# Moving one of two differences of x from VectorE to GpSimd in a residual block of two 3x3 convolutions

## The chip, the core and the metric

One core of a Trainium2 chip runs the whole kernel in one launch. The metric is the device time in microseconds, the median of the runs. Of the engines, TensorE (PE; PEld are its weight loads) multiplies matrices, VectorE (DVE), ScalarE (ACT) and GpSimd (POOL) work element by element, and SyncE (SP) issues most of the transfers. Each engine has an instruction stream of its own; they meet at semaphores only, all of them written by hand in this kernel.

## The reference

The input x is 32 images of 64 channels of 56 x 56 in float32. Both convolutions are 3x3 with padding 1 and 64 channels in and out.

```python
def _bn(x, gamma, beta, mean, var):
    inv = gamma * jax.lax.rsqrt(var + EPS)
    return x * inv[None, :, None, None] + (beta - mean * inv)[None, :, None, None]
identity = x
out = jax.nn.relu(_bn(_conv3x3(x, w1, stride=1), g1, b1, m1, v1))
out = _bn(_conv3x3(out, w2, stride=1), g2, b2, m2, v2)
return jax.nn.relu(out + identity)
```

## The kernel before

**Layout.** The 128 partitions are two row parities times 64 channels: a partition holds 28 row pairs of 56 columns of one channel. x_sb has two buffers (XBUFS), one image each, filled by two transfers (one for each row parity). Each convolution is written in a form that saves products along the columns: the input is turned into four column combinations of half width (28 columns), each is multiplied by its own transformed filter, and the results are combined into even and odd output columns. The four combinations of x are:

- the inner pair, x_inner: even plus odd columns (`sum_x`, L392) and odd minus even columns (`difference_x`, L396);
- the outer pair, x_outer: differences of columns two apart (`outer_x`, L407).

Hidden, the relu of conv1, is turned in the same way into t_inner (`sum_hidden` L440, `difference_hidden` L446) and t_outer (`outer_hidden` L454).

**Precision.** TensorE works on pairs of reduced-precision parts: ScalarE rounds a combination to a high part (`high_x` L547, `high_hidden` L568), VectorE subtracts it for the low part (`split_x` L417, `split_hidden` L462), and three products are summed (hi by w_hi, hi by w_lo, lo by w_hi). Only hidden's difference is multiplied in float32 as it is (t_inner by w_mat, at the matmul line L679). All products go to PSUM by halves of an image; a half has four banks.

**From products to output.** ScalarE copies the bank of the inner difference with the bias into z (`copy_sum`, L577 and L578), VectorE joins it with the other inner bank into the even and odd banks (`join`, L431), TensorE adds the outer products onto them, and ScalarE takes the relu: into hidden for conv1 (`relu_hidden`, L583), into out_sb for conv2 (`relu_out`, L606). The residual is added through x_inner: ScalarE writes half the sum and minus half the difference into the conv2 banks (`residual`, L557) before TensorE adds to them. x_inner has four buffers (TBUFS) for this, x_outer has one.

**Order of the work.** Each engine runs the same numbered steps s. In step s, image s+1 is prepared (sum, difference, outer combination, rounding), conv1 of image s is done, image s-1 goes from hidden to conv2, and image s-2 ends. Inside a step each engine's order is written out by hand, with a semaphore wait ahead of each operation. VectorE's step, cut to its middle:

```python
                if now:
                    join(1, s, 0, (2, s - 2))
                if ahead:
                    sum_x(s + 1, ka)
                if last:
                    split_hidden("t1", s - 1, kl % 2)
                if ahead:
                    difference_x(s + 1, ka)
                if now:
                    join(1, s, 1, (2, s - 2))
                if ahead:
                    outer_x(s + 1, ka)
```

Ahead of these stand the second conv2 join of image s-2 and the three combinations of hidden of image s-1; behind them split_hidden of t_outer, split_x of the inner pair, the first conv2 join of image s-1 and split_x of the outer pair. SP's step loads image s+2 into the buffer that outer_x(s) has read for the last time (it waits for tx_ready["outer"], L317), then stores image s-2. GpSimd works only in the prologue: it clears tiles, scales the filters (`scale_matrix`, L243), builds the inner filters of layer 2 (L214 to L216) and their low part (`low_weights`, L257). ScalarE's `high_x` waits for tx_ready, which `difference_x` increments for the inner pair, and ScalarE's first steps have the high part of layer 2's weights (L250) just ahead of `high_x("inner", 1)`.

Of the kernel before, what the change touches and what calls it, by code (L numbers as in the profile page):

```python
# [1 line left out]

# [5 lines left out]
ALU = mybir.AluOpType  # L45
# [3 lines left out]
XBUFS = 2  # L49
TBUFS = 4  # L50
# [10 lines left out]
def residual_block(nc, x, w1, w2, params, out):  # L61
# [14 lines left out]
    with ExitStack() as ctx:  # L76
# [3 lines left out]
        def sem(name):  # L80
            return ctx.enter_context(nc.semaphore(name))
# [60 lines left out]
            {which: sem(f"{what}_{which}") for which in sets} for what in ("filled", "mat", "whi", "wlo"))  # L142

        tx_ready = {"inner": sem("tx_inner"), "outer": sem("tx_outer")}
        xhi_ready = {"inner": sem("xhi_inner"), "outer": sem("xhi_outer")}
        xlo_ready = {"inner": sem("xlo_inner"), "outer": sem("xlo_outer")}

# [152 lines left out]
        @block.sync  # L300
        def _(sp):
            def store(n, half):
                j0, j1 = HALF2[half]

                wait(sp, out_ready, 2 * n + half + 1)
                for parity in range(2):
                    sp.dma_start(out_rows[n, parity][:, j0:j1, :],
                                 out_sb[parity * C:parity * C + C, half]).then_inc(stored[half], 16)

            sp.dma_start(bn[:], params).then_inc(bn_in, 16)  # L310
            load_parity(sp, 0, 0, 0)
            sp.dma_start(w_raw[2][:], w2).then_inc(w_in[2], 16)

            def step(s, k):
                if not isinstance(s, int) or s + 2 < N:

                    wait(sp, tx_ready["outer"], s + 3 - XBUFS)  # L317
                    for parity in range(2):
                        load_parity(sp, s + 2, k + 2, parity)
                if there_is(s, s - 2):  # L320
                    store(s - 2, 0)
                    store(s - 2, 1)

            run(sp, step)

            for half in range(2):
                sp.wait_ge(stored[half], 32 * N)

        @block.gpsimd
        def _(pool):  # L330


            nc.gpsimd.memset(wmat[1][:], 0.0).then_inc(mat_zeroed, 1)
            nc.gpsimd.memset(x_sb[:, :, :, 0:1], 0.0).then_inc(x_zeroed, 1)
            nc.gpsimd.memset(x_sb[:, :, :, W + 1:W + 2], 0.0).then_inc(x_zeroed, 1)
            for t in (x_hi, x_lo):
                for b in range(2):
                    for row in (0, NQ + 1):
                        nc.gpsimd.memset(t[:, b, :, row, :].bitcast(F32), 0.0).then_inc(zeroed, 1)
            nc.gpsimd.memset(hidden[:], 0.0).then_inc(zeroed, 1)  # L340
            nc.gpsimd.memset(wmat[2][:], 0.0).then_inc(mat_zeroed, 1)


            after, row = chain(pool, bn_step[2]), slice(2 + C, 2 + 2 * C)

            pool.wait_ge(inv_ready, 2)
            newton_step(pool, after, row)
            after(pool.tensor_tensor(inv[:, row], inv[:, row], bn[:, 8 + C:8 + 2 * C], ALU.mult))
            pool.tensor_scalar(inv[:, row], inv[:, row], 0.5, None, ALU.mult).then_inc(scale_ready[2], 1)


            scale_matrix(pool, "inner1")
            scale_matrix(pool, "outer1")


            after = chain(pool, prep[2])

            pool.wait_ge(w_in[2], 16)
            double_inner_filters(pool, 2, after)
            scale_matrix(pool, "all2")  # L360
            low_weights(pool, "all2")

        @block.vector
        def _(dve):
# [22 lines left out]
            def sum_x(n, k):  # L387


                dve.wait_ge(x_in[k % XBUFS], (n - k % XBUFS) * (32 // XBUFS) + 32)  # L390
                wait(dve, res_ready, 2 * (n - TBUFS) + 2)
                nc.vector.tensor_tensor(x_inner[:, k, 0], x_columns(k, 0), x_columns(k, 1), ALU.add)  # L392

            def difference_x(n, k):

                nc.vector.tensor_tensor(x_inner[:, k, 1], x_columns(k, 1), x_columns(k, 0),  # L396
                                        ALU.subtract).then_inc(tx_ready["inner"], 1)

            def outer_x(n, k):

# [63 lines left out]
            def step(s, k):  # L464
                ahead, now, last = there_is(s, s + 1), there_is(s, s), there_is(s, s - 1)
                ka, kl = (k + 1) % 4, (k + 3) % 4
                if is_step(s, N):

                    sum_hidden(N - 1, 0)
                    difference_hidden(N - 1, 0)  # L470
                    outer_hidden(N - 1, 0)
                    sum_hidden(N - 1, 1)
                    join(2, N - 2, 1, before_conv2(N - 2))
                    split_hidden("t1", N - 1, kl % 2, 0)
                    split_hidden("outer", N - 1, kl % 2, 0)
                    outer_hidden(N - 1, 1)
                    difference_hidden(N - 1, 1)
                    split_hidden("t1", N - 1, kl % 2, 1)
                    join(2, N - 1, 0, before_conv2(N - 1))
                    split_hidden("outer", N - 1, kl % 2, 1)  # L480
                    return

                if there_is(s, s - 2):
                    join(2, s - 2, 1, before_conv2(s - 2))
                if last:
                    sum_hidden(s - 1)
                    difference_hidden(s - 1)
                    outer_hidden(s - 1)
# [4 lines that stand above are left out]
                    sum_x(s + 1, ka)  # L493
                if last:
                    split_hidden("t1", s - 1, kl % 2)
                if ahead:
                    difference_x(s + 1, ka)
                if now:
                    join(1, s, 1, (2, s - 2))

# [3 lines that stand above are left out]
                    split_hidden("outer", s - 1, kl % 2)  # L504
                if is_step(s, -1):
                    low_weights(dve, "inner1")
                if ahead:
                    split_x("inner", s + 1, ka)

                if last:  # L510
                    join(2, s - 1, 0, before_conv2(s - 1))
                if is_step(s, -1):
                    low_weights(dve, "outer1")
                if ahead:
                    split_x("outer", s + 1, ka)
# [4 lines left out]
        def _(act):  # L520
# [21 lines left out]
            def high_x(which, n, k):  # L542
                full, places = x_full(which, k)

                act.wait_ge(tx_ready[which], n + 1)
                wait(act, outer[1], 2 * (n - 1))
                nc.scalar.activation(x_part(x_hi, k, places), full, ACT.Copy).then_inc(xhi_ready[which], 1)  # L547

# [240 lines left out]
```

## Time and profile before

| | |
|---|---|
| median of 3 runs | 620.58 us (619.97 to 620.64) |
| span of the profiled execution | 618.4 us |
| granted TensorE clock | 0.99 of full speed over the span |
| TensorE, weight loads | 594.2 us (96%), 540.8 us (87%) |
| VectorE | 585.9 us (95%) |
| ScalarE | 476.4 us (77%) |
| GpSimd | 21.0 us (3%) |
| DMA | 52.26 MB, mean 85 GB/s |

The page gives one profiled execution by its span, from the first to the last instruction on the core; no separate time of that execution is given. The median of the runs stands 2.2 us above that span. A busy share is an average over the whole span. Matmuls overlap in TensorE's pipe, so its share is no measure of how near it is to its peak. In a timeline, the start of an operation and the start of the next one on its engine are nearer together than its duration by some 0.1 us, since the next one's start overlaps the last one's end.

### The profile page before, as it was taken

Reading aid. Unit: us, or ns where it says so; the run is one execution under the profiler, and the core shown is the slowest. Engines: PE = TensorE matmul, PEld = TensorE weight load, DVE = VectorE, ACT = ScalarE, POOL = GpSimd, SP = SyncE. Lnnn points to the kernel's source line nnn. Section 1 sums busy time; section 2 is a strip of 40 time slices with the busy share of each in tenths; the row PEclk is TensorE's granted clock in tenths of the full one; section 3 lists DMA queues with packets and bytes.
Section 4 is the critical chain, followed back from the end, with each engine's and each line's share of the span. In section 5 each row is a group of like instructions: output and inputs, shape, how many; then the busy total and the mean of one; then the engine's idle time right before and its main releaser. Section 6 shows DMA issues by size and latency. Waiting matters only on the chain.

```text
span 618.4 us, 8933 instructions
## 1 busy us (share of the span) xinstructions
PE 594.2 (96%) x2962; PEld 540.8 (87%) x2962; DVE 585.9 (95%) x475; ACT 476.4 (77%) x730; POOL 21.0 (3%) x30
## 2 busy tenths in 40 slices
PE   6779999999999999999999999999999999999996
PEld 2668988999998899898898999889989889899885
DVE  6899999999999999999999999999999999999963
ACT  5677878877787877787887778787778788777874
POOL 7600000000000000000000000000000000000000
PEclk9789999999999999999999999999999999999999
DMA  9445666445656546566645565654655664552125
GB/s 151 52 53 79 89 95 103 83 76 88 94 78 104 93 74 92 78 86 96 104 77 79 86 94 80 104 91 73 93 80 83 99 104 77 79 83 45 29 53 104
DMA packets 232891, 52.26 MB, mean 85 GB/s; under 512 B 232496, under 2 KB 232624, under 8 KB 232880
## 3 DMA queue, kind: packets, MB, share of 16 engines
q1 hardware_dynamic: 230928, 51.42, 54.1%
q10 hardware_dynamic: 1952, 0.70, 0.6%
q8 instruction: 6, 0.10, 0.1%
q14 instruction: 5, 0.04, 0.0%
HBM read 26.42 MB, written 25.69 MB: 84 GB/s over the span
## 4 chain that ended last, share of the span: by engine, by line
PE 52%; DVE 24%; issue 12%; ACT 8%; DVEq 0%; ACTq 0%; POOL 0%
PE psum L679 52%; DVE psum L431 8%; DVE x_lo L417 8%; DVE h_lo L462 6%; ACT out_sb L606 3%; DVE x_outer L407 3%; ACT hidden L583 1%; ACT psum L557 1%; ACT z L577 1%; ACT z L578 1%; ACT x_hi L547 1%; ACT h_hi L568 1%; ACT w_mat L531 0%; POOL g_t L216 0%; DVE x_inner L392 0%
## 5 line engine op out<-in xcount | busy, mean ns | idle before, releaser
L679 PE MATMUL psum<-x_hi,w_hi 128*128 128x420 f32 (+1 forms) x512 | 181.4, 354 | 13.1 <-DVE x_lo L417 8.9
L679 PE MATMUL psum<-x_hi,w_lo 128*128 128x420 f32 (+1 forms) x512 | 179.2, 350 | 0.0
L679 PE MATMUL psum<-x_lo,w_hi 128*128 128x420 f32 (+1 forms) x512 | 178.5, 349 | 0.0
L431 DVE TENSOR_TENSOR psum<-psum,z 128x784 f32<-128x784 f32 (+1 forms) x128 | 127.8, 998 | 16.8 <-ACT out_sb L606 11.8
L679 PEld LDWEIGHTS psum<-x_hi,w_hi 128*128 128x128 f32 x512 | 97.2, 190 | 24.0 <-issue 16.4
L407 DVE TENSOR_TENSOR x_outer<-x_sb 128x1568 f32<-128x1568 f32 x32 | 98.7, 3084 | 0.0
L679 PEld LDWEIGHTS psum<-x_hi,w_lo 128*128 128x128 f32 x512 | 97.4, 190 | 0.9
L679 PEld LDWEIGHTS psum<-x_lo,w_hi 128*128 128x128 f32 x512 | 97.2, 190 | 0.9
L679 PE MATMUL psum<-t_inner,w_mat 128*128 128x392 f32 x256 | 94.7, 492 | 1.1 <-ACT psum L557 1.1
L606 ACT ACTIVATE out_sb<-psum 128x784 f32<-128x784 f32 x64 | 57.2, 894 | 48.6 <-PE psum L679 48.5
L577 ACT ACTIVATE z<-psum,bias 128x392 f32<-128x392 f32 (+1 forms) x128 | 75.6, 590 | 23.8 <-PE psum L679 21.2
L679 PE MATMUL psum<-h_lo,w_hi 128*128 128x392 f32 x256 | 87.3, 341 | 0.0
L679 PE MATMUL psum<-h_hi,w_hi 128*128 128x392 f32 x256 | 87.2, 341 | 0.0
L679 PE MATMUL psum<-h_hi,w_lo 128*128 128x392 f32 x256 | 87.0, 340 | 0.0
L583 ACT ACTIVATE hidden<-psum 64x56 f32<-64x56 f32 (+2 forms) x128 | 61.1, 504 | 18.7 <-PE psum L679 18.3
L578 ACT ACTIVATE z<-psum,bias 128x392 f32<-128x392 f32 (+1 forms) x128 | 75.5, 590 | 0.0
L679 PEld LDWEIGHTS psum<-t_inner,w_mat 128*128 128x128 f32 x256 | 47.9, 188 | 19.4 <-issue 1.4
L557 ACT ACTIVATE psum<-x_inner 128x392 f32<-128x392 f32 x128 | 59.3, 503 | 5.0 <-DVE psum L431 3.7
L679 PE MATMUL psum<-t_hi,w_hi 128*128 128x392 f32 x128 | 62.8, 491 | 0.0
L454 DVE TENSOR_TENSOR t_outer<-hidden 128x1624 f32<-128x1624 f32 (+2 forms) x33 | 59.5, 1803 | 0.0
L462 DVE TENSOR_TENSOR h_lo<-t_outer,h_hi 128x1624 fp32r<-128x1624 f32 (+2 forms) x33 | 59.0, 1787 | 0.3 <-ACT h_hi L568 0.3
L417 DVE TENSOR_TENSOR x_lo<-x_outer,x_hi 128x1568 fp32r<-128x1568 f32 x32 | 57.5, 1798 | 0.0
(69 smaller groups left out, 751.0 us busy)
## 6 DMA issues: line engine op xcount, KB each, us to landing
out_dram<-out_sb SPq DMA_DIRECT2D x128, 196.0 KB, 3.3
x_sb<-x_dram SPq DMA_DIRECT2D x63, 392.0 KB, 6.6
x_sb<-x_dram ACTq DMA_DIRECT2D x1, 392.0 KB, 7.2
w_raw<-w_dram ACTq DMA_DIRECT2D x1, 288.0 KB, 4.1
w_raw<-w_dram SPq DMA_DIRECT2D x1, 288.0 KB, 8.4
bn<-params_dram SPq DMA_DIRECT2D x1, 132.0 KB, 3.6
```

The source lines that it names most:

```text
L407: nc.vector.tensor_tensor(x_outer[:].rearrange("p s j q -> p j q s"), rows[:, :, 0:W].rearrange("p j (q s) -> p j q s", s=2), rows[:, :, 2 ...
L417: nc.vector.tensor_tensor(x_part(x_lo, k, places), full, x_part(x_hi, k, places).bitcast(F32), ALU.subtract).then_inc(xlo_ready[which], 1)
L431: nc.vector.tensor_tensor(psum[:, half, EVEN:ODD + 1, 0:width], t1, z[:, half, :, 0:width], ALU.add).then_inc(joined[conv], 1)
L454: nc.vector.tensor_tensor(t_outer[:, :, rows], hid_cols[:, :, rows, 0:WQ], hid_cols[:, :, rows, 1:WQ + 1], ALU.subtract).then_inc(th_ready ...
L462: nc.vector.tensor_tensor(lo, full, hi.bitcast(F32), ALU.subtract).then_inc(hlo_ready[which], 1)
L547: nc.scalar.activation(x_part(x_hi, k, places), full, ACT.Copy).then_inc(xhi_ready[which], 1)
L557: ins = nc.scalar.activation(psum[:, half, bank, 0:width], x_inner[:, k, i, j0:j1, :].rearrange("p j q -> p (j q)"), ACT.Copy, scale=share)
L577: nc.scalar.activation(z[:, half, 0, 0:width], t2, ACT.Identity, bias=bias[:, conv - 1:conv])
L578: nc.scalar.activation(z[:, half, 1, 0:width], t2, ACT.Identity, bias=bias[:, conv - 1:conv], scale=-1.0).then_inc(z_ready[conv], 1)
L583: return nc.scalar.activation(hid_data[rows, :, pairs, 0:WQ], sums[rows], ACT.Relu)
L606: nc.scalar.activation(out_sb[:, half].rearrange("p j (q s) -> p s j q", s=2), psum[:, half, EVEN:ODD + 1, 0:(j1 - j0) * WQ].rearrange("p ...
L679: ins = nc.tensor.matmul(psum[:, half, bank, 0:width], w[:, i, far, :], moving, start=not onto and at == 0, stop=at == len(todo) - 1, skip ...
```

## The change

GpSimd computes the difference of the inner pair of x for every image, VectorE only the sum. GpSimd's difference waits for the image's load and for the residual of the image four back, and increments a new semaphore, difference_ready. VectorE's sum now increments tx_ready["inner"]. ScalarE's rounding of the inner pair waits for both, and so does SP's load into the x buffer (there, for the outer combination and for the difference). On GpSimd the difference of image 0 stands between the scalings of the inner and of the outer filters of layer 1, and the others follow behind all of its prologue.

```diff
@@ -142,6 +105,7 @@
             {which: sem(f"{what}_{which}") for which in sets} for what in ("filled", "mat", "whi", "wlo"))
 
         tx_ready = {"inner": sem("tx_inner"), "outer": sem("tx_outer")}
+        difference_ready = sem("difference_ready")
         xhi_ready = {"inner": sem("xhi_inner"), "outer": sem("xhi_outer")}
         xlo_ready = {"inner": sem("xlo_inner"), "outer": sem("xlo_outer")}
 
@@ -315,6 +279,7 @@
                 if not isinstance(s, int) or s + 2 < N:
 
                     wait(sp, tx_ready["outer"], s + 3 - XBUFS)
+                    wait(sp, difference_ready, s + 3 - XBUFS)
                     for parity in range(2):
                         load_parity(sp, s + 2, k + 2, parity)
                 if there_is(s, s - 2):
@@ -349,9 +314,16 @@
             pool.tensor_scalar(inv[:, row], inv[:, row], 0.5, None, ALU.mult).then_inc(scale_ready[2], 1)
 
 
+            def difference_x(n, k):
+
+                pool.wait_ge(x_in[k % XBUFS], (n - k % XBUFS) * (32 // XBUFS) + 32)
+                wait(pool, res_ready, 2 * (n - TBUFS) + 2)
+                pool.tensor_tensor(x_inner[:, k, 1], x_columns(k, 1), x_columns(k, 0),
+                                   ALU.subtract).then_inc(difference_ready, 1)
+
             scale_matrix(pool, "inner1")
+            difference_x(0, 0)
             scale_matrix(pool, "outer1")
-
 
             after = chain(pool, prep[2])
 
@@ -359,6 +331,12 @@
             double_inner_filters(pool, 2, after)
             scale_matrix(pool, "all2")
             low_weights(pool, "all2")
+
+            def step(s, k):
+                if there_is(s, s + 1) and not is_step(s, -1):
+                    difference_x(s + 1, (k + 1) % 4)
+
+            run(pool, step)
 
         @block.vector
         def _(dve):
@@ -389,12 +367,8 @@
 
                 dve.wait_ge(x_in[k % XBUFS], (n - k % XBUFS) * (32 // XBUFS) + 32)
                 wait(dve, res_ready, 2 * (n - TBUFS) + 2)
-                nc.vector.tensor_tensor(x_inner[:, k, 0], x_columns(k, 0), x_columns(k, 1), ALU.add)
-
-            def difference_x(n, k):
-
-                nc.vector.tensor_tensor(x_inner[:, k, 1], x_columns(k, 1), x_columns(k, 0),
-                                        ALU.subtract).then_inc(tx_ready["inner"], 1)
+                nc.vector.tensor_tensor(x_inner[:, k, 0], x_columns(k, 0), x_columns(k, 1),
+                                        ALU.add).then_inc(tx_ready["inner"], 1)
 
             def outer_x(n, k):
 
@@ -493,8 +467,6 @@
                     sum_x(s + 1, ka)
                 if last:
                     split_hidden("t1", s - 1, kl % 2)
-                if ahead:
-                    difference_x(s + 1, ka)
                 if now:
                     join(1, s, 1, (2, s - 2))
 
@@ -543,6 +515,8 @@
                 full, places = x_full(which, k)
 
                 act.wait_ge(tx_ready[which], n + 1)
+                if which == "inner":
+                    act.wait_ge(difference_ready, n + 1)
                 wait(act, outer[1], 2 * (n - 1))
                 nc.scalar.activation(x_part(x_hi, k, places), full, ACT.Copy).then_inc(xhi_ready[which], 1)
```

**VectorE, the middle of step 2** (the first in the loop). x_inner<-x_sb are the sum (L392) and the difference (L396), psum<-psum,z the joins of conv1, t_lo the low part of hidden's sum. Before:

```order
L431 TENSOR_TENSOR psum<-psum,z 128x2x420 [waits out_ready,inner1]
L390 ISA
L173 ISA [waits x_in1]
L392 TENSOR_TENSOR x_inner<-x_sb 128x784 [waits res_ready]
L462 TENSOR_TENSOR t_lo<-t_inner,t_hi 128x812 [waits hhi_t1]
L396 TENSOR_TENSOR x_inner<-x_sb 128x784
L426 REGISTER_ALU
L427 ISA [waits z1_ready]
L431 TENSOR_TENSOR psum<-psum,z 128x2x392 [waits out_ready,inner1]
L173 REGISTER_ALU
L407 TENSOR_TENSOR x_outer<-x_sb 128x784x2 [waits xlo_outer]
```

With the change (line numbers of the new file, where the sum is L370, the join L405, the outer combination L381):

```order
L405 TENSOR_TENSOR psum<-psum,z 128x2x420 [waits out_ready,inner1]
L368 ISA
L137 ISA [waits x_in1]
L370 TENSOR_TENSOR x_inner<-x_sb 128x784 [waits res_ready]
L436 TENSOR_TENSOR t_lo<-t_inner,t_hi 128x812 [waits hhi_t1]
L400 REGISTER_ALU
L401 ISA [waits z1_ready]
L405 TENSOR_TENSOR psum<-psum,z 128x2x392 [waits out_ready,inner1]
L137 REGISTER_ALU
L381 TENSOR_TENSOR x_outer<-x_sb 128x784x2 [waits xlo_outer]
```

The second x_inner<-x_sb is gone between t_lo and the second join; all else keeps its order, and no wait of VectorE is new.

**GpSimd, from its first weight scaling on.** w_mat<-w_mat,inv is scale_matrix, g_sum and g_t are layer 2's inner filters, w_lo is low_weights. Before:

```order
L243 TENSOR_TENSOR w_mat<-w_mat,inv 128x512 [waits scale1_ready,filled_inner1]
L243 TENSOR_TENSOR w_mat<-w_mat,inv 128x2x256 [waits scale1_ready,filled_outer1]
L214 TENSOR_TENSOR g_sum<-w_raw 128x192 [waits w2_in]
L215 TENSOR_TENSOR g_t<-g_sum,w_raw 128x192 [waits prep2]
L216 TENSOR_TENSOR g_t<-g_sum,w_raw 128x192
L243 TENSOR_TENSOR w_mat<-w_mat,inv 128x1024 [waits scale2_ready,filled_all2,prep2]
L257 TENSOR_TENSOR w_lo<-w_mat,w_hi 128x1024 [waits whi_all2]
```

With the change (x_inner<-x_sb, L321 of the new file, is the difference):

```order
L207 TENSOR_TENSOR w_mat<-w_mat,inv 128x512 [waits scale1_ready,filled_inner1]
L321 TENSOR_TENSOR x_inner<-x_sb 128x784 [waits x_in0]
L207 TENSOR_TENSOR w_mat<-w_mat,inv 128x2x256 [waits scale1_ready,filled_outer1]
L178 TENSOR_TENSOR g_sum<-w_raw 128x192 [waits w2_in]
L179 TENSOR_TENSOR g_t<-g_sum,w_raw 128x192 [waits prep2]
L180 TENSOR_TENSOR g_t<-g_sum,w_raw 128x192
L207 TENSOR_TENSOR w_mat<-w_mat,inv 128x1024 [waits scale2_ready,filled_all2,prep2]
L221 TENSOR_TENSOR w_lo<-w_mat,w_hi 128x1024 [waits whi_all2]
L321 TENSOR_TENSOR x_inner<-x_sb 128x784 [waits x_in1]
L321 TENSOR_TENSOR x_inner<-x_sb 128x784 [waits x_in0]
```

The difference of image 0 stands behind the first scaling, those of images 1 and 2 behind w_lo, and 29 more follow, one for each later image; each waits for its image's x_in, and from image 4 on for res_ready too.

## Rows read from the trace of the kernel before

**Rows 1.** the page, busy time, share and instructions of each engine

```profile
PE 594.2 (96%) x2962; PEld 540.8 (87%) x2962; DVE 585.9 (95%) x475; ACT 476.4 (77%) x730; POOL 21.0 (3%) x30
```

**Rows 2.** waits of VectorE, 100 to 560 us: us in total, times, longest

```profile
DVE psum L431 <- ACT out_sb L606: 8.3, 25, 0.4
```

**Rows 3.** groups of VectorE, 45 to 540 us: busy, mean ns, idle before

```profile
L417 DVE TENSOR_TENSOR x_lo<-x_inner,x_hi 128x1568 fp32r<-128x1568 f32 x27 | 48.0, 1778 | 0.0
...
L396 DVE TENSOR_TENSOR x_inner<-x_sb 128x784 f32<-128x784 f32 x27 | 26.4, 979 | 0.0
```

**Rows 4.** timeline of VectorE, one image: start us, us, what, idle before

```profile
298.61 0.98 DVE L431 TENSOR_TENSOR psum<-psum,z 128x784 f32<-128x784 f32 x1 [0.34 <-ACT out_sb L606]
299.50 3.02 DVE L407 TENSOR_TENSOR x_outer<-x_sb 128x1568 f32<-128x1568 f32 x1
...
309.26 1.01 DVE L440 TENSOR_TENSOR t_inner<-hidden 128x812 f32<-128x812 f32 x1
310.17 1.02 DVE L446 TENSOR_TENSOR t_inner<-hidden 128x812 f32<-128x812 f32 x1
311.09 1.87 DVE L454 TENSOR_TENSOR t_outer<-hidden 128x1624 f32<-128x1624 f32 x1
312.85 1.06 DVE L431 TENSOR_TENSOR psum<-psum,z 128x840 f32<-128x840 f32 x1
...
315.58 1.00 DVE L396 TENSOR_TENSOR x_inner<-x_sb 128x784 f32<-128x784 f32 x1
316.94 0.98 DVE L431 TENSOR_TENSOR psum<-psum,z 128x784 f32<-128x784 f32 x1 [0.35 <-ACT out_sb L606]
```

**Rows 5.** timeline of ScalarE in the same image

```profile
313.94 0.92 ACT L557 ACTIVATE psum<-x_inner 128x392 f32<-128x392 f32 x2
315.93 0.90 ACT L606 ACTIVATE out_sb<-psum 128x784 f32<-128x784 f32 x1 [1.07 <-PE psum L679]
```

**Rows 6.** timeline of TensorE's weight loads in the same image

```profile
306.91 0.19 PEld L679 LDWEIGHTS psum<-x_hi,w_hi 128*128 128x128 f32 x1 [0.48 <-issue]
...
315.56 0.19 PEld L679 LDWEIGHTS psum<-t_inner,w_mat 128*128 128x128 f32 x1
```

**Rows 7.** x_sb on SP, 303.3 to 304.5 us: load of the second half, its landing

```profile
L295 SPq DMA_DIRECT2D x_sb<-x_dram x1: 809/809/809, 303.5 to 303.5; - x1
...
DMA to landing us min/median/max: 6.6/6.6/6.6
```

**Rows 8.** timeline of GpSimd, the prologue

```profile
11.15 5.26 POOL L243 TENSOR_TENSOR w_mat<-w_mat,inv 128x512 f32<-128x512 f32 x2
...
19.48 1.04 POOL L216 TENSOR_TENSOR g_t<-g_sum,w_raw 128x192 f32<-128x192 f32 x1
...
27.00 2.41 POOL L257 TENSOR_TENSOR w_lo<-w_mat,w_hi 128x1024 fp32r<-128x1024 f32 x1 [2.01 <-ACT w_hi L250]
```

**Rows 9.** timeline of VectorE, the prologue and first steps

```profile
10.88 1.00 DVE L396 TENSOR_TENSOR x_inner<-x_sb 128x784 f32<-128x784 f32 x1
11.80 3.78 DVE L407 TENSOR_TENSOR x_outer<-x_sb 128x1568 f32<-128x1568 f32 x1
...
19.98 2.18 DVE L417 TENSOR_TENSOR x_lo<-x_outer,x_hi 128x1568 fp32r<-128x1568 f32 x1
...
26.75 0.98 DVE L431 TENSOR_TENSOR psum<-psum,z 128x784 f32<-128x784 f32 x1
27.63 4.54 DVE L407 TENSOR_TENSOR x_outer<-x_sb 128x1568 f32<-128x1568 f32 x1
...
35.45 1.00 DVE L440 TENSOR_TENSOR t_inner<-hidden 128x812 f32<-128x812 f32 x1
```

**Rows 10.** timeline of ScalarE, the first steps

```profile
26.87 1.52 ACT L547 ACTIVATE x_hi<-x_inner 128x1568 fp32r<-128x1568 f32 x1
28.29 0.93 ACT L583 ACTIVATE hidden<-psum 64x56 f32<-64x56 f32 x2
...
33.74 1.01 ACT L583 ACTIVATE hidden<-psum 64x56 f32<-64x56 f32 x2
```


## The prediction

> **What bounds the kernel now.** I read the busy shares first [rows 1]: TensorE 594.2 us and VectorE 585.9 us of a 618.4 us span, so either could be the bound. The waits of VectorE from 100 to 560 us [rows 2] decide more: in each of 25 images its psum join waited for ScalarE's out_sb, 8.3 us in all. An engine that waits in every image is not what sets the time alone. Then I followed one image. It takes 18.33 us (join at 298.61, the same join at 316.94) [rows 4]. The idle time of VectorE, 0.35 us, stands just before that join (conv1, second half), and the difference to be taken away, 1.00 us at 315.58, stands just ahead of the idle time. The join waits for relu_out, which ran 315.93 to 316.83 on ScalarE [rows 5], and relu_out waited for TensorE. After the join VectorE runs x_outer, h_lo, x_lo and the conv2 join without a pause; TensorE waits for that join, with a gap of 0.48 us at 306.91 [rows 6]. So the loop is TensorE, relu_out, join, x_outer and what follows, TensorE. The difference isn't in it.
>
> **What is removed.** One VectorE operation per image, 0.98 us [rows 3], 0.9 us from its start to the next one. Its cover is the wait for relu_out: with it gone, VectorE could start the join at 315.58 and would wait for 316.94 all the same. Value: zero. What VectorE gets is room, 1.36 us between 315.58 and 316.94. The semaphore of the inner pair moves onto the sum, still on VectorE, at no cost.
>
> **What is added: a reader beside VectorE.** The new operation waits for x_in of its own image and for res_ready of an image four back. Nothing else holds it, so GpSimd runs a whole step ahead of VectorE: at the moment a load lands. The load goes out when x_outer is through; its second half was issued at 303.5 and landed 6.6 us later, at 310.1 [rows 7]. That is 0.05 us before VectorE's difference of hidden at 310.17, while the sum of 309.26 still runs [rows 4]. A little earlier or later makes no matter: each of sum, difference and outer_hidden (309.26 to 312.96) reads two SBUF tiles.
>
> Do the two engines get in each other's way? The prologue shows it [rows 8, 9]. While GpSimd had its two scalings of 512 columns in hand (5.26 us together), x_outer took 3.78 us instead of 3.02. While it had w_lo (27.00, 2.41 us), x_outer took 4.54. While it had 192-column operations, x_lo took 2.18 us instead of 1.78 [rows 3]. And GpSimd waits in its turn: a tiny operation of 192 columns is 1.04 us long at 19.48. So they take turns, an operation at a time, and VectorE loses the whole reading time of each GpSimd operation that gets in between.
>
> How long is that for 784 columns? Three rows:
> - 192 columns: 2.18 - 1.78 = 0.40 us, 2.1 ns a column; for 784, 1.63 us.
> - 1024 columns: reading began by 27.00 and x_outer (start 27.63) lost 1.52, so it ended near 29.15: 2.15 us, 2.1 ns a column; for 784, 1.65 us. By the whole recorded 2.41 us it would be 1.85.
> - 512 columns, one operand a repeated row of 64: 3.78 - 3.02 = 0.76 us; for 784, 1.16 us.
>
> The new operation has two full operands, as the first two have: I take **1.65 us**, with 1.16 and 1.85 as ends. The Trainium skill (GPSIMD Engine Reference, 3.1 Elementwise) gives 4497 ns for a two-operand add of 2048 columns; as an estimate that is 1.72 us here, and with it the sum below would be 2 us more. The trace's 2.1 ns a column agrees within 5%.
>
> **What 1.65 us does to a step.** It falls ahead of outer_hidden, thus ahead of the first conv1 join (312.85) [rows 4]. Three roads lead on from there:
> - VectorE itself, to the second conv1 join: 1.36 us of room (above).
> - ScalarE: residual waits for the first conv1 join (ended 313.91, residual 313.94 to 314.86), and relu_out stands behind it. It could have started at 314.79, operations on ScalarE overlapping by some 0.07 us, and started at 315.93 [rows 5]: room 1.14.
> - TensorE: its fp32 products wait for residual. They began at 315.56 [rows 6], 0.64 us after they could (314.86 and 0.06 for the semaphore). Behind them TensorE has the gap of 0.48 us. Room 0.64 + 0.48 = 1.12.
>
> The shortest room counts: 1.65 - 1.12 = 0.53 us a step. Images 4 to 31 are loaded in steady steps, 28 of them: 28 x 0.53 = **14.8 us**.
>
> **The start.** In the prologue GpSimd has a queue of its own, and the change puts image 0's difference between two weight scalings and image 1's behind all its weight work.
> - With no difference at 10.88, x_outer(0) starts there, holds the reading to 13.8, and the first scaling, which got in at 11.8, is 2.0 us late. The difference of image 0 adds 1.65. VectorE is idle for some of it, and the work of 192 columns (its last at 19.48) ends about 1.1 us late [rows 8, 9].
> - So w_lo asks at 28.1 instead of 27.00, just after x_outer(1) has begun (27.9); x_outer holds to 30.8, w_lo runs to about 33.1, the difference of image 1 to 34.9.
> - x_hi inner on ScalarE, at 26.87 before, waits for that to 34.9 and holds up all behind it: relu_hidden at 28.29, x_hi outer, the second relu_hidden (33.74 before; 34.9 + 1.4 + 0.9 + 1.4 = 38.7 now) [rows 10]. VectorE's first sum of hidden, 35.45 before [rows 9], follows x_lo of the outer pair (38.7 to 40.5): 5.0 us late. The removed difference (-0.9) and image 3's (which meets the unhindered join and then the sum of x, +0.8) nearly cancel.
>
> I take **4.9 us**. Lower end: if w_lo still ran at 27.00 to 29.4, difference 1 would end at 31.2 and the second relu_hidden start at 35.0, 1.3 us late. SP's new wait costs nothing beyond this: from image 2 on GpSimd is done a whole step before x_outer, which SP waits for anyway. The end of the kernel has no x work: zero.
>
> **Sum.** 14.8 + 4.9 = 19.7 us on the profiled span of 618.4, that is 638.1; the median of 620.58 lies 2.2 us above that span, so **640.3 us**. Ends: 1.16 us lies on the room of 1.12, so 28 x 0.04 = 1 and 1.3 make 623; 1.85 gives 28 x 0.73 = 20.4, and with 6 us at the start 647.
>
> **The rivals.**
> 1. *Faster: VectorE is the bound.* For it: 95% busy, and TensorE's gap stands where it waits for a VectorE join. If the 0.89 us came through in every image, it could give at most TensorE's gap, 29 x 0.48 = 13.9 us: 620.6 - 13.9 = 606.7. It needs the GpSimd reads to cost nothing and relu_out to come earlier. Against it: the join waited for out_sb in all 25 images looked at, behind the place of the removal. It decides from a reading time under 0.3 us, and the rows say 0.76 or more. 4%.
> 2. *The reading is covered.* If the landing fell 2 us later, GpSimd would get in behind outer_hidden, beside the conv1 join, which reads one tile in SBUF and one in PSUM. w_lo at 27.00 began during such a join (26.75), which wasn't lengthened. VectorE would lose 1.65 - 0.94 = 0.71, less than the room, and so too with a reading time near 1.16: only the start remains, 620.6 + 1.3 to 4.9 = 622 to 626. The Trainium skill (SBUF — State Buffer, Who interferes with whom) says that an instruction of VectorE with at most one SBUF input doesn't contend with GpSimd; the trace agrees, 0.98 us for the join. Against it: the landings sit at 10.6 us behind x_outer's start, and outer_hidden's end 13.4 behind it. 14%.
> 3. *GpSimd is slower than its dense rows.* x is read in steps of two elements, which no row shows on GpSimd. At 2.2 us reading, 28 x 1.08 = 30 and 6 for the start: 657. 12%.
> 4. *GpSimd never gets between back-to-back VectorE operations* and only starts in VectorE's gaps or joins. It has a whole step in hand, so this is rival 2's time, 622 to 626. Against it: operations of 192 columns did get in between x_lo and w_lo. 5%.
>
> **The numbers.** The forecast, 630 to 648, has 65%; 3 and what lies above, 12%; 2 and 4, 19%; 1, 4%. The likeliest is 640.3. The range of 8 in 10 takes in most of the covered cases and not much of rival 3: 624 to 649. Over 0.2% (1.2 us, about what a measurement of this kernel can tell from no change) slower: 92%; within it: 4%, the low end of the covered cases; faster: 4%.
>
> **What the profile would show.** Right: GpSimd's operations some 10.7 us behind each start of x_outer, each next to a VectorE operation of 2.5 to 3.5 us where it was 1.0 or 1.87; an image of about 18.85 us; waits of TensorE for residual (psum by ScalarE) where there was hardly one; the first sum of hidden near 40 us. Wrong: images of 18.3 us with unstretched operations (rivals 2, 4), or under 18.3 (rival 1); a stretch over 2 us (rival 3).

## Result and profile after

The changed kernel takes 629.44 us (median of 4 runs, 629.09 to 629.80) against 620.50 for the kernel before (4 runs). The ratio is 1.0147, 95% interval 1.0133 to 1.0162: slower by 8.9 us, where 19.7 was forecast. The span of the profiled execution went from 618.4 to 627.0 us, 8.6 more.

The page of the changed kernel, and the waits of all engines from 100 to 560 us:

```profile
PE 592.7 (95%) x2962; PEld 540.5 (86%) x2962; DVE 587.6 (94%) x443; ACT 474.8 (76%) x730; POOL 99.3 (16%) x62
```

```profile
POOL x_inner L321 <- DMA x_sb<-x_dram: 400.4, 25, 17.5
ACT psum L531 <- DVE psum L405: 28.4, 21, 1.5
...
PE psum L653 <- ACT psum L531: 7.3, 20, 0.4
DVE psum L405 <- ACT out_sb L580: 4.5, 5, 0.9
```

VectorE's busy time has not fallen [rows 1]: it has 32 operations fewer, and 587.6 us against 585.9. The wait for out_sb, 25 times in rows 2, comes 5 times. TensorE waits for ScalarE's psum (the residual) 20 times; before, it never did in this stretch.

One image on VectorE, and GpSimd beside it:

```profile
305.73 3.02 DVE L381 TENSOR_TENSOR x_outer<-x_sb 128x1568 f32<-128x1568 f32 x1
...
316.47 1.00 DVE L420 TENSOR_TENSOR t_inner<-hidden 128x812 f32<-128x812 f32 x1
317.39 3.14 DVE L428 TENSOR_TENSOR t_outer<-hidden 128x1624 f32<-128x1624 f32 x1
320.45 1.03 DVE L405 TENSOR_TENSOR psum<-psum,z 128x840 f32<-128x840 f32 x1
...
324.25 3.04 DVE L381 TENSOR_TENSOR x_outer<-x_sb 128x1568 f32<-128x1568 f32 x1
```

```profile
316.47 2.35 POOL L321 TENSOR_TENSOR x_inner<-x_sb 128x784 f32<-128x784 f32 x1 [16.17 <-DMA x_sb<-x_dram]
```

The x_outer of 305.73 is followed by the next at 324.25, 18.52 us on. GpSimd's operation starts 10.74 us after x_outer did, as its load lands, in the same instant as VectorE's difference of hidden. It waits for that one's end, and t_outer, the next on VectorE, takes 3.14 us instead of 1.87 [rows 4]: 1.3 us longer, the reading of 784 columns. Of the 29 images loaded in steps, 20 stretch t_outer so, 2 the difference of hidden (2.3 us instead of 1.0). In the other 7 GpSimd waits for the end of t_outer, reads beside the conv1 join, which keeps its length, and only 0.4 us is left for the sum of x (1.33 to 1.38 instead of 0.96). One of these:

```profile
279.59 1.02 DVE L420 TENSOR_TENSOR t_inner<-hidden 128x812 f32<-128x812 f32 x1
280.50 1.87 DVE L428 TENSOR_TENSOR t_outer<-hidden 128x1624 f32<-128x1624 f32 x1
282.26 1.06 DVE L405 TENSOR_TENSOR psum<-psum,z 128x840 f32<-128x840 f32 x1
283.20 1.36 DVE L370 TENSOR_TENSOR x_inner<-x_sb 128x784 f32<-128x784 f32 x1
```

```profile
279.87 3.86 POOL L321 TENSOR_TENSOR x_inner<-x_sb 128x784 f32<-128x784 f32 x1 [16.38 <-DMA x_sb<-x_dram]
```

The moment of the landing doesn't tell the two kinds apart. By the profile GpSimd's operation began 0.41 to 0.92 us ahead of t_outer in the 20 images that stretch it, and 0.63 to 0.93 us ahead of it in 6 of the 7 others (in the seventh, image 3 at the start, t_outer already ran). So GpSimd, though it asked in time, was sometimes passed over at t_outer's start; what decides it is open.

Where the 8.6 us came in is read from x_outer, 32 times in each kernel (its line's first and last start; the third start from the timeline):

```profile
L381 DVE TENSOR_TENSOR x_outer<-x_sb x32: 2907/3021/3060, 10.8 to 582.6; 128x1568 f32<-128x1568 f32 x32
```

```profile
47.28 3.02 DVE L381 TENSOR_TENSOR x_outer<-x_sb 128x1568 f32<-128x1568 f32 x1
```

The third x_outer starts at 47.28, before at 43.55: **3.7 us at the start**. The last starts at 582.6, before at 573.9: 29 images took 535.3 us instead of 530.3, 18.46 each instead of 18.29: **5.0 us in the steady steps**. The 22 images with a stretched operation carry nearly all of it: they take 18.50 us in the mean, 0.21 more each, 4.6 us in all.

The start itself:

```profile
11.07 3.47 POOL L207 TENSOR_TENSOR w_mat<-w_mat,inv 128x512 f32<-128x512 f32 x1
...
27.66 5.03 POOL L221 TENSOR_TENSOR w_lo<-w_mat,w_hi 128x1024 fp32r<-128x1024 f32 x1 [2.04 <-ACT w_hi L214]
32.65 2.94 POOL L321 TENSOR_TENSOR x_inner<-x_sb 128x784 f32<-128x784 f32 x2
```

```profile
34.23 1.51 ACT L521 ACTIVATE x_hi<-x_inner 128x1568 fp32r<-128x1568 f32 x1 [6.65 <-POOL x_inner L321]
```

The first scaling (L207) waited for x_outer(0), 11.07 to 14.54. w_lo (L221) waited for x_outer(1), 5.03 us long instead of 2.41 [rows 8]. The two differences behind it are through at 34.1 and 35.6, and ScalarE's x_hi, at 26.87 before [rows 10], started at 34.23, with 6.65 us idle ahead of it.

### The profile page after: what moved, and what is told of

It is laid out like the page before. It is cut to its first block, busy times and chain, and to the rows that moved or that the text cites. A ratio compares the mean times of both kernels' runs of the same rounds, so it can differ in the third digit from the quotient of the medians.

```text
span 627.0 us, 9030 instructions
## 1 busy us (share of the span) xinstructions
PE 592.7 (95%) x2962; PEld 540.5 (86%) x2962; DVE 587.6 (94%) x443; ACT 474.8 (76%) x730; POOL 99.3 (16%) x62
## 4 chain that ended last, share of the span: by engine, by line
PE 76%; ACT 7%; DVE 7%; issue 5%; POOL 1%; DVEq 0%; ACTq 0%; POOLq 0%
PE psum L653 76%; DVE psum L405 4%; ACT z L551 2%; ACT psum L531 2%; ACT z L552 2%; DVE x_lo L391 1%; DVE x_outer L381 1%; DVE h_lo L436 1%; ACT x_hi L521 0%; ACT out_sb L580 0%; POOL w_mat L207 0%; POOL x_inner L321 0%; POOL g_t L180 0%; DVEq L401 0%; DVE t_inner L414 0%
## 5 line engine op out<-in xcount | busy, mean ns | idle before, releaser
L653 PE MATMUL psum<-x_hi,w_hi 128*128 128x420 f32 (+1 forms) x512 | 179.6, 351 | 14.8 <-DVE x_lo L391 13.9
L321 POOL TENSOR_TENSOR x_inner<-x_sb 128x784 f32<-128x784 f32 x32 | 76.4, 2390 | 451.1 <-DMA x_sb<-x_dram 451.1
L405 DVE TENSOR_TENSOR psum<-psum,z 128x784 f32<-128x784 f32 (+1 forms) x128 | 127.5, 996 | 15.6 <-ACT out_sb L580 8.6
L653 PE MATMUL psum<-t_inner,w_mat 128*128 128x392 f32 x256 | 96.4, 499 | 9.4 <-ACT psum L531 9.4
L381 DVE TENSOR_TENSOR x_outer<-x_sb 128x1568 f32<-128x1568 f32 x32 | 96.6, 3019 | 0.0
L428 DVE TENSOR_TENSOR t_outer<-hidden 128x1624 f32<-128x1624 f32 (+2 forms) x33 | 85.4, 2587 | 0.0
L653 PEld LDWEIGHTS psum<-t_inner,w_mat 128*128 128x128 f32 x256 | 46.4, 188 | 34.3 <-issue 14.5
L391 DVE TENSOR_TENSOR x_lo<-x_inner,x_hi 128x1568 fp32r<-128x1568 f32 x32 | 57.3, 1791 | 6.3 <-ACT x_hi L521 6.3
```

The source lines that it names most:

```text
L321: pool.tensor_tensor(x_inner[:, k, 1], x_columns(k, 1), x_columns(k, 0), ALU.subtract).then_inc(difference_ready, 1)
L381: nc.vector.tensor_tensor(x_outer[:].rearrange("p s j q -> p j q s"), rows[:, :, 0:W].rearrange("p j (q s) -> p j q s", s=2), rows[:, :, 2 ...
L391: nc.vector.tensor_tensor(x_part(x_lo, k, places), full, x_part(x_hi, k, places).bitcast(F32), ALU.subtract).then_inc(xlo_ready[which], 1)
L405: nc.vector.tensor_tensor(psum[:, half, EVEN:ODD + 1, 0:width], t1, z[:, half, :, 0:width], ALU.add).then_inc(joined[conv], 1)
L428: nc.vector.tensor_tensor(t_outer[:, :, rows], hid_cols[:, :, rows, 0:WQ], hid_cols[:, :, rows, 1:WQ + 1], ALU.subtract).then_inc(th_ready ...
L653: ins = nc.tensor.matmul(psum[:, half, bank, 0:width], w[:, i, far, :], moving, start=not onto and at == 0, stop=at == len(todo) - 1, skip ...
```

## Experiments

Each is compared with the kernel before, run on the same chip. Edits are shown by their main lines, against the changed kernel unless said otherwise. "Mean image" is the mean distance from the third x_outer to the last.

### The removal alone

```diff
 (against the kernel before; images 0 to 2 only)
-                if ahead:
+                if is_step(s, -1) or is_step(s, 0) or is_step(s, 1):
                     difference_x(s + 1, ka)
```

From image 3 on the sum increments the semaphore of the inner pair in the difference's place.

> The kernel before, with VectorE's difference of x computed for images 0 to 2 only; buffer 3 of x_inner's difference is cleared once, and every later image uses what stands in its buffer (output wrong by that, matrix work the same). GpSimd does nothing new. This is the removal alone. Theory (the difference stands in the wait for relu_out, so the removal is worth nothing): as before, within 0.2% (619.5 to 621.5), an image 18.3 us, VectorE idle about 1.2 us ahead of the second conv1 join. Rival (VectorE is the bound and 0.9 us an image comes back): 607 to 612.

Measured: 619.69 us against 620.25, ratio 0.9991 (0.9982 to 1.0000). Its waits of VectorE, 100 to 560 us, and the join on its timeline:

```profile
DVE psum L434 <- ACT out_sb L609: 30.0, 25, 1.2
```

```profile
316.66 0.98 DVE L434 TENSOR_TENSOR psum<-psum,z 128x784 f32<-128x784 f32 x1 [1.21 <-ACT out_sb L609]
```

The wait for out_sb has grown from 0.35 to 1.21 us [rows 4], and the image is 18.3 us as before. The 0.9 us went into that wait. Taking the difference off VectorE is worth 0.6 us here, and the interval reaches from nothing to 1.1 us.

### Where the two costs are

Images 0 and 1 back on VectorE, GpSimd from image 2 on:

```diff
-            difference_x(0, 0)
 ...
-                if there_is(s, s + 1) and not is_step(s, -1):
+                if is_step(s, 1):
+                    pool.wait_ge(difference_ready, 2)
+                if there_is(s, s + 1) and not (is_step(s, -1) or is_step(s, 0)):
 ...
+                if is_step(s, -1) or is_step(s, 0):
+                    difference_first(s + 1, ka)
                 if now:
                     join(1, s, 1, (2, s - 2))
```

> The changed kernel, with the differences of images 0 and 1 back on VectorE in their old place; GpSimd does images 2 to 31. Theory (two costs: 3.7 us at the start from the place in GpSimd's queue, 5.0 us from the reading in steady steps): 629.4 - 3.7 = 625.7, x_outer of image 2 near 43.5 us again, steady images still 18.46 us. Rival (the start is hidden later, all comes from the steady steps): 629.

Measured: 626.24 us, ratio 1.0098 (1.0083 to 1.0114). The third x_outer started at 43.95, the mean image was 18.47 us. The start's cost is gone, the steady one has stayed.

GpSimd's reading moved to where VectorE waits:

```diff
                 wait(pool, res_ready, 2 * (n - TBUFS) + 2)
+                wait(pool, hlo_ready["t1"], n - 1)
```

> The changed kernel, with one more wait on GpSimd: the difference of image n starts only when VectorE is done with t_lo (low part of hidden's sum) of image n-2, so that it reads while VectorE waits for relu_out, 1.36 us of room for a reading of 1.30. Theory (only the place of the reading costs): steady images back to 18.28 us, the start's 3.7 us stay, 624.3. Rival (a GpSimd operation beside VectorE costs wherever it is): 629 or more.

Measured: 624.49 us, ratio 1.0069 (1.0055 to 1.0082); third x_outer at 46.92, mean image 18.32 us. One operation beside the other, VectorE and GpSimd:

```profile
300.53 1.02 DVE L437 TENSOR_TENSOR t_lo<-t_inner,t_hi 128x812 fp32r<-128x812 f32 x1
302.80 0.98 DVE L406 TENSOR_TENSOR psum<-psum,z 128x784 f32<-128x784 f32 x1 [1.25 <-ACT out_sb L581]
303.69 3.01 DVE L382 TENSOR_TENSOR x_outer<-x_sb 128x1568 f32<-128x1568 f32 x1
```

```profile
301.63 1.49 POOL L322 TENSOR_TENSOR x_inner<-x_sb 128x784 f32<-128x784 f32 x1 [16.68 <-DVE t_lo L437]
```

GpSimd reads from 301.63 to about 302.9, in VectorE's pause and the first 0.1 us of the join, and nothing on VectorE is stretched. The same work on the same engines costs nothing there; the images from the fifth x_outer on take 18.29 us, as before the change.

Both edits:

> Both edits: images 0 and 1 on VectorE, and GpSimd's later ones behind t_lo. Theory: both costs gone, 620.5 within 1.2, nothing gained by the change even then. Rival (VectorE as the bound): under 616. Rival (a third cost): 623 or more.

Measured: 620.23 us against 620.25, ratio 1.0002 (0.9993 to 1.0011). The two costs account for the whole change, and with both gone nothing has been gained.

### The room

Half of the rows for GpSimd, the other half on VectorE in the old place:

```diff
-                pool.tensor_tensor(x_inner[:, k, 1], x_columns(k, 1), x_columns(k, 0),
+                pool.tensor_tensor(x_inner[:, k, 1, 0:NQ // 2], x_columns(k, 1)[:, 0:NQ // 2], x_columns(k, 0)[:, 0:NQ // 2],
```

> The changed kernel, with GpSimd taking 14 of the 28 row pairs of each difference and VectorE the other 14 in the old place. Theory (a reading costs only beyond 1.12 us of room): the reading is some 0.7 us, steady images 18.28 to 18.30 us, and of the start's 3.7 us some 2.5 to 3.2 are left: 623 to 624. Rival (the cost follows the work of GpSimd): half of 8.9 us, 625; rival (whatever VectorE loses is lost): above 626.

Measured: 623.18 us, ratio 1.0047 (1.0031 to 1.0064), mean image 18.29 us. VectorE's timeline has t_outer stretched to 2.49 us:

```profile
314.40 2.49 DVE L431 TENSOR_TENSOR t_outer<-hidden 128x1624 f32<-128x1624 f32 x1
```

This is so in 13 of the 27 images between the 4th and the 31st x_outer; in the others GpSimd read beside the join. The 13 take 18.30 us, the others 18.27, the kernel before 18.29: a loss of 0.65 us ahead of the first conv1 join costs no time. The remaining 3.3 us are the start (third x_outer at 46.83).

Each difference twice:

```diff
+                wait(pool, difference_ready, n)
+                pool.tensor_tensor(spare[:], x_columns(k, 1), x_columns(k, 0), ALU.subtract)
                 pool.tensor_tensor(x_inner[:, k, 1], x_columns(k, 1), x_columns(k, 0),
```

> The changed kernel, with each difference computed twice by GpSimd, first into a spare tile (with a wait for its own operation before), then into its place. Theory (turns by whole operations; one with a PSUM operand doesn't take part): the first reading stretches hidden's difference or t_outer by 1.30, the second waits for the end of t_outer and reads beside the first conv1 join, so that only 0.4 of it falls on the sum of x; loss 1.3 + 0.4 = 1.7 an image, 0.6 beyond the room, 17 us, and about 6 at the start: 642 to 645. Rival (the join takes part too, or both readings count): 2.6 - 1.12 = 1.5 an image, 660 to 670.

Measured: 639.69 us, ratio 1.0320 (1.0302 to 1.0337), 2 to 5 us under the forecast of my theory and far from the rival's. VectorE in one image:

```profile
324.81 1.85 DVE L431 TENSOR_TENSOR t_outer<-hidden 128x1624 f32<-128x1624 f32 x1
...
327.51 1.34 DVE L373 TENSOR_TENSOR x_inner<-x_sb 128x784 f32<-128x784 f32 x1
328.78 2.29 DVE L439 TENSOR_TENSOR t_lo<-t_inner,t_hi 128x812 fp32r<-128x812 f32 x1
```

In 25 of 28 images the first reading ran beside the conv1 join and took 0.36 from the sum of x, the second took 1.30 from t_lo: 1.66 us an image, as expected, in other places than expected. The mean image was 18.65 us, 0.37 over the one before where I had counted 0.6. That fits a loss behind the first conv1 join, which meets only VectorE's own room of 1.36 us (1.66 - 1.36 = 0.30) and not the shorter one by way of the residual; VectorE has no wait left in these images. Two errors stand against each other in this forecast: the steady images lost 10.6 us and not 17, and the start 8.3 us (third x_outer at 51.88) and not 6.

### The price of a reading

GpSimd subtracts other operands of the same size, in the same place:

```diff
-                pool.tensor_tensor(x_inner[:, k, 1], x_columns(k, 1), x_columns(k, 0),
+                pool.tensor_tensor(x_inner[:, k, 1], x_sb[:, k % XBUFS, :, 1:WQ + 1], x_sb[:, k % XBUFS, :, WQ + 1:W + 1],
```

> The changed kernel, with GpSimd subtracting the right half of each row from the left half (both dense) in place of odd and even columns (every second element); output wrong by that. Measures the reading. Theory A (784 columns of two operands of one tile cost 1.3 us, dense or not): t_outer or hidden's difference 1.3 us longer in most steps, time as the changed kernel, 629. Theory B (dense costs 2.1 ns a column as the prologue seemed to say, the step of two is what made it cheap): 1.65 us longer, images 18.8 us, 638.

In the next, GpSimd takes `wmat[2]` and `w_lo[2]`, the first 784 columns of each, as operands from image 1 on:

> The changed kernel, with GpSimd's operation from image 1 on subtracting 784 columns of w_lo from 784 of w_mat (two dense tiles, as in the prologue's w_lo) in place of x's columns; output wrong by that. Theory A (784 columns of two operands cost 1.3 us, whatever they are): as the changed kernel. Theory B (two separate tiles cost more, the prologue's 2.1 ns a column): stretched by 1.65 us, 638.

```diff
-                pool.tensor_tensor(x_inner[:, k, 1], x_columns(k, 1), x_columns(k, 0),
+                pool.tensor_tensor(x_inner[:, k, 1, 0:NQ - 1], x_columns(k, 1)[:, 1:NQ], x_columns(k, 1)[:, 0:NQ - 1],
```

> The changed kernel, with GpSimd subtracting the even columns of a row pair from the even columns of the next one (27 x 28 = 756 columns, both operands in steps of two, 58 elements apart); output wrong by that, the last row of the difference stays zero. Two explanations of 1.30 us against the dense 1.70. Theory A (it is the two operands next to each other in memory that is cheap): 2.17 ns a column, t_outer stretched by 1.6 us. Theory B (a step of two is cheap by itself): 1.66 ns a column, stretched by 1.25 us.

`x_columns(k, 1)` are the odd columns, not the even ones as this text says; the layout that it tests is the same.

One run of each: 641.70, 632.42 and 645.75 us. Their whole times are single values; what is read from them is the length of t_outer, which each trace has 13 to 24 times in its stretched form. t_outer on VectorE in the dense one, in the one with two tiles and in the one with rows:

```profile
323.90 3.57 DVE L428 TENSOR_TENSOR t_outer<-hidden 128x1624 f32<-128x1624 f32 x1
```

```profile
322.09 3.58 DVE L434 TENSOR_TENSOR t_outer<-hidden 128x1624 f32<-128x1624 f32 x1
```

```profile
307.08 3.86 DVE L429 TENSOR_TENSOR t_outer<-hidden 128x1624 f32<-128x1624 f32 x1
```

And GpSimd's first operation, which began while VectorE was idle, in the changed kernel, the dense one and the one with rows:

```profile
14.50 1.49 POOL L321 TENSOR_TENSOR x_inner<-x_sb 128x784 f32<-128x784 f32 x1
```

```profile
14.27 1.89 POOL L321 TENSOR_TENSOR x_inner<-x_sb 128x784 f32<-128x784 f32 x1
```

```profile
14.80 2.14 POOL L322 TENSOR_TENSOR x_inner<-x_sb 128x756 f32<-128x756 f32 x1
```

(t_outer unstretched is 1.85 us, its usual length in the changed kernel.)

| operands | stretch of t_outer | columns | ns a column |
|---|---|---|---|
| even and odd columns (the change) | 3.14 - 1.85 = 1.29 us | 784 | 1.65 |
| two halves of a row, dense | 3.57 - 1.85 = 1.72 | 784 | 2.19 |
| two tiles, dense | 3.58 - 1.85 = 1.73 | 784 | 2.21 |
| odd columns of two neighbouring row pairs | 3.86 - 1.85 = 2.01 | 756 | 2.66 |

So the rate of the prologue's rows, 2.1 ns a column, holds for dense operands. The change's own operands, odd and even columns that stand next to each other, cost a quarter less. It isn't the step of two: with the same step and the operands a row apart the price is 2.66, above both my theories. The dense kernel had a mean image of 18.85 us and 641.7 us in all: within 1.4 us of the time forecast for the change, with the operands that the forecast had priced. The kernel with two tiles has the same price and was 9 us faster, because 16 of its 29 operations were passed over and fell beside the join, against 4 in the dense one and 7 in the changed kernel.

With the images sorted so, the three prices give the room. Of the 27 images between the 4th and the 31st x_outer, those with a stretched operation took 18.50 us in the changed kernel, 18.93 in the dense one and 19.20 in the one with rows, 0.21, 0.64 and 0.91 more than before. Taken from their stretches of 1.29, 1.72 and 2.01 this leaves 1.08, 1.08 and 1.10 us.

### A version that beats both

If a loop through relu_out, the join, x_outer, h_lo, x_lo and the conv2 join sets the image, one of its parts can be moved out of it. h_lo is needed only later. It can be cut into its two planes: one stays in its place, while ScalarE still has x_hi of the inner pair in hand (315.00 to 316.53 in the new kernel, where x_lo starts at 316.77), and the other goes behind the first conv2 join (against the kernel before):

```diff
                 if last:
-                    split_hidden("outer", s - 1, kl % 2)
+                    split_outer(s - 1, kl % 2, 0)
 ...
                 if last:
                     join(2, s - 1, 0, before_conv2(s - 1))
+                    split_outer(s - 1, kl % 2, 1)
```

TensorE waits for the end of that low part once more in the last step.

> The kernel before (difference on VectorE), with VectorE's h_lo (low part of t_outer) cut into its two planes: the second is done behind the first conv2 join, so x_lo of the inner pair and that join, on which TensorE waits, come 0.9 us earlier. TensorE waits for the end of that operation once more in the last step. Theory (the loop by relu_out and these operations sets the image, with TensorE's gap of 0.48 us and VectorE's of 0.4 behind it): images 17.9 to 18.0 us, 610 to 613. Rival (both engines are full and the gap comes back elsewhere): 619 to 621.

Measured: **609.11 us**, ratio 0.9819 (0.9806 to 0.9833) to the kernel before, 11.1 us faster than it and some 20 faster than the change. The mean image is 17.95 us; the list of waits from 100 to 560 us has none of TensorE and none of VectorE left:

```profile
ACT t_hi L577 <- DVE t_inner L440: 38.5, 26, 1.6
ACT psum L566 <- DVE psum L431: 18.0, 25, 0.8
ACT hidden L592 <- PE psum L688: 13.7, 26, 0.6
ACT out_sb L615 <- PE psum L688: 12.5, 25, 0.6
ACT z L586 <- PE psum L688: 0.9, 6, 0.2
```

The cut on top of the kernel with both edits (images 0 and 1 on VectorE, later ones behind t_lo):

> The same cut on top of the kernel in which GpSimd does the differences from image 2 on behind t_lo. Now VectorE has no wait in which the reading can hide, and a reading of 1.30 us takes more than the 0.9 us it frees. Theory: VectorE's work 17.0 + 1.3 = 18.3 us an image, 619 to 621, about 9 slower than the cut alone. Rival (the reading hides still): as the cut alone or better, 607 to 612.

Measured: 609.44 us, ratio 0.9827 (0.9814 to 0.9841), the same as the cut alone: my theory missed by 10 us. VectorE and GpSimd:

```profile
308.84 1.00 DVE L442 TENSOR_TENSOR t_lo<-t_inner,t_hi 128x812 fp32r<-128x812 f32 x1
310.60 0.98 DVE L411 TENSOR_TENSOR psum<-psum,z 128x784 f32<-128x784 f32 x1 [0.76 <-ACT out_sb L597]
311.49 3.00 DVE L387 TENSOR_TENSOR x_outer<-x_sb 128x1568 f32<-128x1568 f32 x1
```

```profile
309.99 1.50 POOL L322 TENSOR_TENSOR x_inner<-x_sb 128x784 f32<-128x784 f32 x1 [16.47 <-DVE t_lo L442]
```

With the difference gone VectorE has a wait of 0.76 us for out_sb, and the join behind it (0.89 us from its start to the next) reads one tile in SBUF and goes on beside GpSimd. Both together are more than the reading of 1.3 us, so it is covered whole. I had added the reading to VectorE's work as if the join took part, against what the moved reading had shown.

And the cut on top of the removal alone:

> The cut on top of the kernel with differences for images 0 to 2 only (output wrong by that): what the removal would be worth where VectorE is the bound. Theory (VectorE and TensorE both need about 17.9 us an image then): TensorE takes over as the bound, 17.8 to 17.9, 607 to 611, at most 3 below the cut alone. Rival (VectorE is the only bound): 0.9 us an image below the cut, under 595.

Measured: 608.72 us, ratio 0.9817 (0.9803 to 0.9830), mean image 17.90 us. The removal is worth 0.4 us here, no more than the runs of either kernel differ among themselves. The wait for out_sb is back on VectorE, while TensorE's matmuls, whose ends are modelled, cover all 460.00 us from 100 to 560 us, as they do with the cut alone (456.69 in the kernel before).

## Why the prediction was wrong

The sign, the mechanism and nearly all places were right; the size was off by a factor of two, 8.9 us instead of 19.7.

- **The removal, worth zero**: right, 0.6 us by itself, in an interval of 0 to 1.1.
- **GpSimd starts as the load lands, 10.7 us behind x_outer**: right, 10.74. **They take turns by whole operations**: right, t_outer stretched by 1.3 us in 20 of 29 images. But a request ahead of t_outer did not always get the next turn; 6 times it waited for t_outer too. The Trainium skill (SBUF — State Buffer, Who interferes with whom) has the rule for it, a VectorE instruction with two SBUF inputs contends with a GpSimd instruction that reads SBUF; the trace agrees. So it does with the page's exception for one SBUF input: the conv1 joins beside GpSimd's readings kept their length, 1.02 to 1.08 us for the one of 840 columns as in the kernel before, 0.98 for the one of 784 columns in the two kernels that read behind t_lo.
- **"I take 1.65 us"**: this is the step that failed. The reading took 1.30 us. The price came from operations with dense operands, and the new one reads odd and even neighbours. The text named the step of two as unseen, but only as a risk upwards, in rival 3. With 1.30 the same sum gives 28 x (1.30 - 1.12) = 5.0 us, and 5.0 was measured; that it agrees to the tenth is luck, since 22 of the 28 images were hindered and each lost 0.21, not 0.18. The loss beyond the room is a small difference, so an error of 0.35 us in the reading made one of 10 us in the sum. The estimate by the Trainium skill's figure (GPSIMD Engine Reference, 3.1 Elementwise), 1.72 us, is right for the dense operands tried above (1.72) and wrong for the change's.
- **The room of 1.12 us**: right within 0.04. A loss of 0.65 cost nothing; 1.29, 1.72 and 2.01 left a room of 1.08 to 1.10 in the images that they hit. The 0.06 us for a semaphore in the forecast's sum stands in no row; where TensorE waited for the conv2 join before, its next weight load started 0.12 us after that join's end (306.79 to 306.91), and with 0.12 the sum is 1.06. TensorE waits for the residual as forecast.
- **The start, "I take 4.9 us"**: 3.7. The chain of waits was the one forecast, with shorter links. With the shorter reading the work of 192 columns ended 0.6 us late, not 1.1 (its last operation started at 20.10 instead of 19.48), and the first difference behind w_lo was through at 34.1, not 34.9. The first sum of hidden came 4.2 us late (39.69), not 5.0. "Nearly cancel" was wrong: the removed difference gave back 0.9 us and image 3's cost only 0.4, which brings 4.2 to 3.7. It was also close: w_lo began 0.05 us behind x_outer(1) (27.66 and 27.61), and in the kernel before, where it began first, it read first.
- **Rivals 2 and 4, the reading beside the join**: it was 7 of 29 images, not all or none, and in 6 of them without the late landing that rival 2 asked for. The forecast let every request in at the next boundary; how many images are spared differs between the kernels above (4 to 16 of 29), and the sum had no term for that.
- The range, 624 to 649, held the time. It was the size claimed for the likeliest case that was wrong, and its own range (630 to 648) just missed 629.4.

What stays open is why operands next to each other are read faster, and what decides whether GpSimd gets the next turn; the runs show that both happen, not how.

## What to carry to other kernels

Look first whether the operation to be moved stands just ahead of a wait on its own engine, as here: the wait then takes up what is freed. Taking half of another operation out of the loop gave 11 us. In this kernel a GpSimd operation beside a VectorE operation with two SBUF inputs was not free parallel work: price its reading as lost VectorE time, and then choose the place where it reads with a semaphore, since the same operation cost 5 us where its data landed and nothing in VectorE's wait. Where a cost is counted beyond some room, the room and the cost must be known within their difference; price it from operands of the same layout, or give it a range that says it isn't known.

## What the hardware showed that I had not expected

GpSimd's reading time for a two-operand subtraction depended on how the operands lie to each other: 1.65 ns a column for odd and even neighbours, 2.2 for dense operands, 2.66 for a step of two with the operands a row apart. A VectorE join with one operand in PSUM kept its length beside any of them (1.02 to 1.08 us for 840 columns), which makes it a place to put GpSimd's work. And a GpSimd operation that asks while VectorE runs back to back may be passed over at the next boundary: with the same lead of 0.6 to 0.9 us it got in there in most images and not in 6 of 29.
